# Four residual layers on one Trainium2 core: layer 2's rank products from fp32 operands in column tiles, and gate and up's step 1 begun behind step 0's first two products

## The reference: what is computed

```
x = x + einsum('bsi,boi->bso', x, w0[ids0])                          # layer 0
x = x + x @ W.T + 2 * (h * gates) @ B                                # layer 1, router over 8 experts, rank 16
x = x + x @ weight.T + bias + 0.5 * (x @ A[ids3]) @ lora_B.T         # layer 2, rank 32
gate = x @ Wg.T + 0.5 * (x @ Ag[ids4].T) @ Bg[ids4].T                # layer 3, rank 16
up   = x @ Wu.T + 0.5 * (x @ Au[ids4].T) @ Bu[ids4].T
act  = silu(gate) * up                                               # 1376 columns, padded to 11 blocks of 128
x = x + act @ Wd.T + 0.5 * (act @ Ad[ids4].T) @ Bd[ids4].T
```

## Time and profile before

| | |
|---|---|
| time, median of 3 runs | 288.58 us (288.47 to 288.65) |
| the profiled execution's own time | 288.6 us |
| its span (first to last instruction) | 286.8 us |
| TensorE busy | 279.4 us, 97% of the span |
| VectorE busy | 227.5 us, 79% |
| ScalarE busy | 158.5 us, 55% |
| GpSimd busy | 45.7 us, 16% |
| chain that ended last | 95% TensorE |

### The profile page before, as it was taken

One profiled execution on the slowest core, in us unless ns is written; L12 is line 12 of the kernel. 1 busy time (PEld: TensorE's weight loads), 2 busy tenths in 40 slices (PEclk: granted clock), 3 DMA queues, 4 the chain that ended last, 5 costly groups with the idle time before them and its releaser, 6 DMA issues.

```text
span 286.8 us, 4499 instructions
## 1 busy us (share of the span) xinstructions
PE 279.4 (97%) x1573; PEld 231.2 (81%) x1573; DVE 227.5 (79%) x341; ACT 158.5 (55%) x256; POOL 45.7 (16%) x67
## 2 busy tenths in 40 slices
PE   7899999999999999999999999999999999999993
PEld 7567878888888778888888888888888888888883
DVE  0698897894746999989686785785789999799990
ACT  2688672512425269775746646646667849952110
POOL 1000000000714502514244044044000000000000
PEclk9999999999999999999999999999999999999999
DMA  6999954007603040030270350330291500000043
GB/s 199 371 401 395 400 181 112 0 0 237 204 0 81 22 125 25 10 139 0 65 228 5 100 193 2 110 111 0 73 336 69 152 0 0 0 2 0 0 181 113
DMA packets 19447, 33.28 MB, mean 116 GB/s; under 512 B 2528, under 2 KB 11232, under 8 KB 19040
## 3 DMA queue, kind: packets, MB, share of 16 engines
q1 hardware_dynamic: 19136, 32.47, 33.2%
q10 hardware_dynamic: 288, 0.52, 0.6%
HBM read 30.89 MB, written 2.10 MB: 115 GB/s over the span
## 4 chain that ended last, share of the span: by engine, by line
PE 95%; DMA 2%; DVE 1%; SPq 1%; issue 0%
PE bank L1617 12%; PE bank L1618 12%; PE bank L1619 12%; PE bank L1494 6%; PE bank L1496 6%; PE bank L1495 6%; PE bank L1757 6%; PE bank L1759 6%; PE bank L1760 6%; PE bank L1599 4%; PE bank L1454 3%; PE bank L1471 2%; PE bank L1478 2%; PE bank L1742 2%; DMA w_raw<-in_w 2%; PE bank L1480 2%
## 5 line engine op out<-in xcount | busy, mean ns | idle before, releaser
L619 ACT ACTIVATE part<-bank 128x512 f32<-128x512 f32 x48 | 28.3, 595 | 44.8 <-PE bank L1619 34.7
L1218 DVE TENSOR_TENSOR part<-bank,part 128x512 f32<-128x512 f32 x44 | 29.2, 683 | 1.4 <-PE bank L1599 1.4
L1143 DVE SCALAR_TENSOR_TENSOR bgu_st<-bgu_st,lo_rows,bgu_raw 128x512 fp32r<-128x512 f32 x22 | 17.3, 824 | 12.1 <-ACT bgu_st L619 12.1
L967 DVE TENSOR_TENSOR w_hl<-w_raw,w_hl 128x512 fp32r<-128x512 f32 x31 | 20.0, 687 | 5.6 <-ACT w_hl L619 5.6
L619 ACT ACTIVATE w_hl<-w_raw 128x512 fp32r<-128x512 f32 x31 | 18.6, 622 | 6.1 <-DMA w_raw<-in_w 6.0
L601 POOL TENSOR_TENSOR s_tmp<-wgu_raw 128x256 f32<-128x256 f32 x11 | 8.4, 762 | 80.7 <-DVE wc_up L967 38.8
L1617 PE MATMUL bank<-xb,wc_gate 128*128 128x512 f32 x48 | 18.9, 394 | 0.0
L1619 PE MATMUL bank<-xb,wc_gate 128*128 128x512 f32 x48 | 18.9, 394 | 0.0
L1618 PE MATMUL bank<-xb,wc_gate 128*128 128x512 f32 x48 | 18.8, 392 | 0.0
L1599 PEld LDWEIGHTS bank<-t_st,bgu_st 128*128 128x128 f32 x88 | 14.7, 188 | 2.8 <-DVE t_st L1208 0.3
L619 ACT ACTIVATE xb<-x_f 128x512 fp32r<-128x512 f32 x14 | 8.8, 626 | 13.4 <-DVE x_f L1088 9.4
(11 more groups left out here) (227 smaller groups left out, 792.1 us busy)
## 6 DMA issues: line engine op xcount, KB each, us to landing
wgu_raw<-in_wgu SPq DMA_DIRECT2D x11, 512.0 KB, 4.4
bgu_raw<-in_bgu SPq DMA_DIRECT2D x40, 128.0 KB, 2.7
w_raw<-in_w SPq DMA_DIRECT2D x16, 256.0 KB, 10.9
w_raw<-in_w SPq DMA_DIRECT2D x3, 1024.0 KB, 6.8
w_raw<-in_w SPq DMA_DIRECT2D x6, 512.0 KB, 10.4
wd_raw<-in_wd SPq DMA_DIRECT2D x4, 704.0 KB, 5.9
x_f<-in_xT SPq DMA_DIRECT2D x6, 256.0 KB, 10.1
bd_raw<-in_bd SPq DMA_DIRECT2D x8, 128.0 KB, 2.8
```

The source lines that it names most:

```text
L619: return act.activation(dst, src, ACT.Copy)
L967: return dve.tensor_tensor(dst, src, hi.bitcast(F32), ALU.subtract)
L1143: return dve.scalar_tensor_tensor(out=st, in0=st.bitcast(F32), scalar=lo_rows16[:, 0:1], in1=raw, op0=ALU.mult, op1=ALU.add)
L1218: dve.tensor_tensor(dst[:], bank[4 * (n % 2) + b][:], dst[:], ALU.add).then_inc(c_added, 1)
```

## The change

In layer 2, `thin` becomes `thin2`: fp32 operands (a2_raw and x_f, no split), 32 columns for each of the four sequences in column tiles of their own, 16 matmuls for each half, as `thin3` has it. It waits for x_sum and not for the split of x; that wait (x_lo) now stands behind it, ahead of `base(2,h,0)`. The selection matmul becomes `spread2`: four fp32 matmuls of 128 columns with a matrix t2_sel that POOL builds. ACT's copy into uv becomes a copy of 128 x 128 (`t2_copy`); its copy of sel_r, the split of A on ACT and DVE, and DVE's two subtractions into uv fall away. POOL's memset of t3_st waits for l2_tm to reach 2 (both halves of `thin2` done), and the load of ad_raw for t2_done.

In gate and up, p1(1) and p2(1) move up to stand right behind p2(0). In ACT's and DVE's queues the operations of step 1's weights and xt(2) move ahead of the copies of layer 3's ranks.

```diff
@@ gpsimd
             pool.wait_ge(l0_tr, B)
-            pool.wait_ge(w12_lo, nth["a2"])
+            pool.memset(t2_sel[:], 0.0).then_inc(t2_sel_step, 1)
+            pool.wait_ge(t2_sel_step, 1)
+            pool.wait_ge(sel_in, 16)
+            for j in range(HB):
+                rows = slice(32 * j, 32 * j + 32)
+                pool.tensor_copy(t2_sel[rows, j], sel_raw[rows, 2 * P:3 * P]).then_inc(t2_sel_step, 1)
+            pool.wait_ge(t2_sel_step, 1 + HB)
             pool.wait_ge(main_done, 8)
...
-            pool.wait_ge(sel_copied, 1)
+            pool.wait_ge(l2_tm, H)
             pool.wait_ge(hi_lo_copied, 1)
             pool.memset(t3_st[:].bitcast(F32), 0.0).then_inc(t3_zeroed, 1)
@@ scalar
-            split_hi("a2")
...
-            def t2_uv_high(h):
+            def t2_copy(h):
                 act.wait_ge(l2_tm, h + 1)
-                high(uv[0:2 * R2, h * HT:(h + 1) * HT], bank[h][0:2 * R2]).then_inc(t2_uv_hi, 1)
+                high(t2_sb[:, h], bank[h][:, 0:S]).then_inc(t2_copied, 1)
...
-            act.wait_ge(sel_in, 16)
-            high(sel_r[:], sel_raw[:, 2 * P:3 * P]).then_inc(sel_copied, 1)
...
             copy_part(0, 0)
+            xt_high(2)
+            wc_high(1, 1)
+            wc_high(1, 2)
+            copy_part(1, 0)
             t3_high(0)
             copy_part(0, 1)
-            xt_high(2)
             t3_copy(1)
-            wc_high(1, 1)
-            wc_high(1, 2)
             bgu_high(0, 1)
-            copy_part(1, 0)
             xt_high(3)
@@ vector
-            split_lo("a2")
...
-            t2_uv_low(0)
...
-            t2_uv_low(1)
...
-            t3_low(0)
-            bgu_low(0, 1)
             for part_of in (1, 2):
                 wc_low(1, part_of)
             xt_low(2)
+            t3_low(0)
+            bgu_low(0, 1)
             xt_low(3)
@@ tensor
-            def thin(h, a_hl, x):
+            def thin2(h):
+
+                pe.wait_ge(x_sum, number(1, h, C - 1) + 1)
+                for c in range(C):
+                    for j in range(HB):
+                        b = HB * h + j
+                        ins = pe.matmul(bank[h][32 * j:32 * j + R2, 0:S], a2_raw[:, b, c], x_f[:, b, c],
+                                        start=(c == 0), stop=(c == C - 1))
+                ins.then_inc(l2_tm, 1)
+
+            def spread2(h):
+
+                pe.wait_ge(t2_copied, h + 1)
                 for j in range(HB):
+                    ins = pe.matmul(bank[2 + h][:, j * S:(j + 1) * S], t2_sel[:, j], t2_sb[:, h], start=True, stop=True)
+                ins.then_inc(t2_done, 1)
...
             for h in range(H):
+                thin2(h)
                 pe.wait_ge(x_lo, x_splits(1, h, C - 1))
-                thin(h, a2_hl, xa).then_inc(l2_tm, 1)
                 base(2, h, 0)
...
             pe.wait_ge(x_sum, number(2, 1, C - 1) + 1)
+            p1(1)
+            p2(1)
             sum_ranks(0)
             p5(0)
             thin3(1)
-            p1(1)
-            p2(1)
             p6(0)
             sum_ranks(1)
             lora_w(0)
```

More of the change, by code:

```diff
@@ L109, in bass_four_residual_layers @@
         a2_raw = at("a2_raw", o_tp + 4 * KB, [B, C, R2])
-        a2_hl = at("a2_hl", o_ad, [B, C, 2, R2], F32R)
+        t2_sel = at("t2_sel", o_ad, [HB, P])
+        t2_sb = at("t2_sb", o_ad + 2 * KB, [H, S])
         b2_raw = at("b2_raw", o_bst + 5 * KB, [D])
         b2_st = at("b2_st", o_bst, [D], F32R)
-        uv = at("uv", o_w0 + 16 * KB, [T], F32R)
         t2_st = at("t2_st", o_w0 + 12 * KB, [T], F32R)
@@ L171, in bass_four_residual_layers @@
         sel_raw = at("sel_raw", o_tp, [4 * P + 1])
-        sel_r = at("sel_r", o_misc, [P], F32R)
         hi_lo = own("hi_lo", [1])
@@ L245, in bass_four_residual_layers @@
         t3_sel_step = sem("t3_sel_step")
-        sel_copied, t2_uv_hi, td_copied = sem("sel_copied"), sem("t2_uv_hi"), sem("td_copied")
+        t2_sel_step, t2_copied, td_copied = sem("t2_sel_step"), sem("t2_copied"), sem("td_copied")
         bgu_hi, silu_done = sem("bgu_hi"), sem("silu_done")
@@ L255, in bass_four_residual_layers @@
         t2_lo, t3_lo = sem("t2_lo"), sem("t3_lo")
-        t2_uv_lo, hi_lo_copied = sem("t2_uv_lo"), sem("hi_lo_copied")
+        hi_lo_copied = sem("hi_lo_copied")
         bgu_ready, act_mul = sem("bgu_ready"), sem("act_mul")
@@ L299, in x_f_tokens @@
             return x_f[:, cols.start // S:cols.stop // S, o]
-        splits = [f"w1_{o}" for o in range(C)] + ["b1", "a2"] + [f"w2_{o}" for o in range(C)] + ["b2"]
+        splits = [f"w1_{o}" for o in range(C)] + ["b1"] + [f"w2_{o}" for o in range(C)] + ["b2"]
         nth = {name: i + 1 for i, name in enumerate(splits)}
@@ L308, in split_views @@
                 return b1_raw[:], b1_hl[:, 0], b1_hl[:, 1]
-            if name == "a2":
-                return a2_raw[:], a2_hl[:, :, :, 0], a2_hl[:, :, :, 1]
             if name == "b2":
@@ L315, in split_views @@
             return raw[:, o], hl[:, 0, o], hl[:, 1, o]
-        split_source = {"b1": (b1_in, 16), "a2": (a2_in, 16 * B), "b2": (b2_in, 16)}
+        split_source = {"b1": (b1_in, 16), "b2": (b2_in, 16)}
         for o in range(C):
@@ L529, in _ @@
             load_wgu(4)
-            sp.wait_ge(l2_tm, 2)
+            sp.wait_ge(t2_done, H)
             for b in range(B):
@@ L571, in _ @@
             pool.wait_ge(t3_sel_step, 1)
-            pool.wait_ge(sel_in, 16)
             for g in range(2):
@@ L729, in xt_high @@
                 high(xt_views(k)[0], tx[k][:]).then_inc(xt_hi, 1)
-            t2_uv_high(0)
-            act.wait_ge(sel_in, 16)
-            high(sel_r[:], sel_raw[:, 2 * P:3 * P]).then_inc(sel_copied, 1)
+            t2_copy(0)
             t2_high(0)
@@ L736, in _ @@
                 x_high(2, 0, o)
-            t2_uv_high(1)
+            t2_copy(1)
             wc_high(0, 0)
@@ L1125, in _ @@
             dve.wait_ge(bias_in, 16)
[L1127 to L1130, removed]
             def t2_low(h):
@@ L1533, in _ @@
                     lora1(h, o)
-            def thin(h, a_hl, x):
-                for j in range(HB):
[L1538 to L1545, removed]
+            def thin2(h):
[8 more added lines that the diff above has]
+                pe.wait_ge(t2_copied, h + 1)
+                for j in range(HB):
+                    ins = pe.matmul(bank[2 + h][:, j * S:(j + 1) * S], t2_sel[:, j], t2_sb[:, h], start=True, stop=True)
+                ins.then_inc(t2_done, 1)
             def delta2(h, o):
@@ L1551, in delta2 @@
                           t2_st[:, h * HT:(h + 1) * HT], start=False, stop=True).then_inc(main_done, 1)
-            pe.wait_ge(w12_lo, nth["a2"])
+            pe.wait_ge(a2_in, 16 * B)
             for h in range(H):
+                thin2(h)
                 pe.wait_ge(x_lo, x_splits(1, h, C - 1))
-                thin(h, a2_hl, xa).then_inc(l2_tm, 1)
                 base(2, h, 0)
[L1559 to L1562, removed]
+                pe.wait_ge(t2_sel_step, 1 + HB)
+                spread2(h)
                 base(2, h, 1)
```

## The result

The changed kernel takes 294.02 us (median of 4 executions, 292.94 to 294.27) against 288.52 us before (median of 4): a ratio of 1.0184, 95% interval 1.0169 to 1.0199, about 5.3 us slower by the ratio (5.5 us between the medians). All four executions are slower than any of before.

A forecast was written before the change was run, and what follows sets the result against it. TensorE, never idle in the changed stretch, was taken as the bound. sum_ranks(1) starting 4.0 us late, with layer 2's 0.3 us only lengthening the wait, on 288.6 us makes 292.6 us; range 290.9 to 294.8 us.

The forecast's parts named there:

- The bound, and that a reordering has nothing to fill: TensorE, busy all 37.00 us from 75 to 112 us, bounds the kernel; reordering its queue can only add a wait.
- The place and the mechanism: Gate and up: TensorE waits at sum_ranks(1) from 111.5 us for t3_low(0), which has three subtractions newly ahead on DVE.
- The size of the wait: At sum_ranks(1): TensorE waits 4.3 us, to 115.8 us, so the second spreading starts 4.0 us later than before.
- the shift ahead of the chain: POOL's moved memset delays form_s(0), ACT's split and DVE's chain behind it by 0.76 us.
- The upper end of 1.4 us: The shift if POOL's memset also waits for a whole DVE operation of 0.7 us; gives 293.3 us.
- Layer 2 on TensorE: thin2 and spread2 in place of the old groups gain 0.2 to 0.4 us for both halves, taken as 0.3.
- the clock's fall: Rival: TensorE's clock drops to half speed behind the wait, costing up to 2.8 us, 295.4 us at most; chance 0.20.
- the likeliest case: The wait at sum_ranks(1) without a fall of the clock: 292.6 us, range 291.2 to 293.3; chance 0.66.
- Its reading of the start: At the program's start, fp32 passes of 0.20 us, against 0.11 us later, show TensorE at 1.2 instead of 2.4 GHz.
- The rest follows as before: Behind sum_ranks(1), everything to the program's end keeps its earlier timing, so its delay of 4.0 us passes on whole.
- rival 2: Gate and up: the wait is there but well shorter, DVE being ahead of the sum; 290 to 291.2 us, chance 0.08.
- Just in time, so no wait yet: p1(1), due at about 103.8 us, needs the last addition to x_f, shifted to 103.7 us; TensorE doesn't wait there.

The follow-up runs named there:

- Run 3: The changed kernel with ACT's and DVE's queues in the order of before, TensorE keeping p1(1) and p2(1) early: 289.84 us, ratio 1.0048.
- run 4: The changed kernel with TensorE's order of before; ACT and DVE keep the new queues: 293.1 us, ratio 1.0159.
- run 2: The kernel before with only the reordering on TensorE, ACT and DVE, layer 2 as before: 292.97 us, ratio 1.0136.
- run 5: The changed kernel with 16 more matmuls on TensorE, moving operand all zeros, in the place of the wait: 291.55 us, ratio 1.0110.
- run 6: The changed kernel with xt_low(2) moved behind the ranks' low parts of half 0 on DVE: 290.6 us, ratio 1.0081.
- run 1: The changed kernel without its reordering: layer 2's part alone, with the memset of t3_st behind l2_tm: 288.25 us, ratio 1.0002.
- run 7: As run 1, but POOL's clearing of the rank tile stands behind step 0's weight sums: 287.56 us, ratio to before 0.9971.
- runs 2 and 9: Run 2, and the kernel before with only POOL's clearing of the rank tile moved behind step 0's weight sums: 287.92 us, ratio 0.9985.

## Why the prediction was right, and what it had wrong

**The bound, and that a reordering has nothing to fill: right.** TensorE waited nowhere in this stretch before; the change gave it a wait.

**The place and the mechanism: right.** TensorE comes to the second spreading at 111.5 us as said and waits for `t3_low(0)`. Run 3 (queues back: no wait there) and run 4 (TensorE's order back: 3.3 us of it) show that the three subtractions and four ACT operations ahead of the ranks make the wait, and run 2 that layer 2 isn't needed for it.

**The size of the wait: 3.67 us late instead of 4.0.** (TensorE idles 3.75 us; the prediction had 4.3.) The chain from `form_t(2)` to the end of `t3_low(0)` was summed as 8.56 us (107.24 to 115.8) and took 8.44 (106.87 to 115.31). The spreading then starts 0.15 us behind its end, which the sum left out. What was too large is the shift ahead of the chain: 0.76 us by the sum, 0.38 measured. The memset began and lasted as said (87.35, 1.82 us), but `form_s(0)` took 2.92 us and not 3.41: its third operation took 0.73 us and not 1.19, since (argued from the timelines, not tried) it no longer fell together with DVE's subtraction of step 0's weights. The upper end of 1.4 us took the Trainium skill's lock of the port pair (SBUF — State Buffer, Terms) to hold for the memset. The trace shows no such delay: the memset took 1.82 us with DVE's subtractions beside it and 1.81 us without. Nor does that page (SBUF: two separate sides) ask for one: it says that a DVE operation with two SBUF inputs contends only with a GpSimd operation that reads SBUF, and a memset reads nothing.

**Layer 2 on TensorE: right.** `thin2` costs 73.54 - 72.20 - 0.23 = 1.11 us and 0.1 us ahead of it, `spread2` 77.18 - 76.06 - 0.23 = 0.89 us:

```profile
72.20 1.08 PE L1532 MATMUL bank<-x_f,a_raw 128*32 128x128 f32 x32
...
73.54 0.40 PE L1486 MATMUL bank<-xa,w_hl 128*128 128x512 f32 x1
...
76.06 1.05 PE L1540 MATMUL bank<-t_sb,t_sel 128*128 128x128 f32 x8
...
77.18 0.40 PE L1486 MATMUL bank<-xa,w_hl 128*128 128x512 f32 x1
```

The two halves together gain 0.2 us, the low end of 0.2 to 0.4.

**The step that failed: the clock's fall was priced as a rival at 0.20, and it is what happened,** in all four executions of the changed kernel. 294.02 us lies above the likeliest case's 291.2 to 293.3; the forecast's range holds it since it reached into this rival. The likeliest case, the wait alone, measures 291.5 us (run 5); the fall brings 1.7 us (run 6), and in some executions 1.1 us more: the changed kernel has a span of 290.7 and 290.8 us where the mean clock is 0.994, and 291.9 us where it is 0.988, the mean of run 4's profiled execution with its longer low stretch. The rival's own price of up to 2.8 us fits the sum. Its reading of the start, that a pass of 0.20 us is one at the low level, is borne out: at a granted clock of 0.50 8 passes of that shape took 1.70 us in run 4, 0.21 us each. That a gap throttles the clock again is the rule cited from the Trainium skill (TensorE: Matmul & The Clock Gate, HAM oscillation), and the traces agree: 0.50 in the windows behind the wait. How long a gap does it was open, and it should have been weighed higher.

**Some luck in the number.** "The rest follows as before" didn't hold at the end: behind the last addition the span is 1.1 us shorter and outside it lie 0.3 us more. Run 5, with the whole wait and no fall, is at 291.55 us where the sum has 292.6, mainly for this reason: its path is 3.84 us longer than before, close to the 4.0 of the sum. In the changed kernel this end took back a part of what the clock cost. A slip without weight is rival 2's time: it leaves the shift of 0.76 us out, and 113.46 - 111.79 gives 290.3 us and not 290.2.

**"Just in time, so no wait yet": right for p1(1) at 103.93, incomplete as an account of the memset.** The copy `t3_copy(0)`, late by the same 0.38 us, isn't waited for in the changed kernel, since p1(1) and p2(1) stand ahead; with the ranks in their old place it costs TensorE about 0.4 us there and 0.2 us at `lora_y(0)` (run 1 against run 7). Having the memset wait for an event for which the next operation waits too moved it from idle time onto a path.

What stays open is the time behind the last addition. It is 3.2 us in the profiled execution of each of the nine kernels that have layer 2's part and 4.3 us in the three that don't (before, runs 2 and 9), so it goes with layer 2's part or with something that comes along with it; which, no run tells. The kernel before has besides two spans, 0.8 us apart, from one execution to the next, and only the longer was profiled.

## What to carry to other kernels

On an engine that waits for nothing, a group moved forward can only make room for a wait: look which semaphore the next group takes, and which queue feeds it; here the damage was done by four ACT and three DVE operations put ahead of one that TensorE needed first. Price a wait of a few microseconds on TensorE as the wait plus some 1.7 to 2.8 us of half clock, and reckon with the fall already at 2 us (3 of 6 executions here); if the wait can't be avoided, even idle multiplications in it are better than nothing (run 5; real work in their place wasn't tried). And an operation that clears or fills memory belongs behind the operation that shares its event, if its own reader comes much later: with layer 2's part that edit gave 0.7 us (run 1 against run 7). The 287.56 us that came of it are 0.3% under the kernel before, but by the profiled executions nearly all of this lies at the end of the program, whose cause is open.

## What the runs showed of the hardware

The clock's fall depends on the execution, not only on the program: it fell in 3 of 6 executions with a gap of 2.1 us, in 3 of 4 with 3.2 us, in 4 of 4 with 3.3 and in 4 of 4 with 3.7 us, and in 5 of 6 with two gaps of 1.6 and 1.4 us and 0.5 us of work between them (the gaps as profiled in one execution of each). Matmuls with an all-zero moving operand held it at 0.999 to 1.000 in 4 of 4. In the profiled executions the low clock came about 1 us into the work (changed kernel) or 1 us ahead of it, with TensorE still idle (run 4), and lasted to 119.8 and to 121.3 us, 4.3 and 5.9 us behind the restart.

The mean clock of an execution counts the end of the program too. In the kernel before (mean 0.999 in the profiled execution) the window from 286 to 287 us has 0.60, 4 us behind its last matmul, where it costs nothing; run 2's 0.991 holds such a stretch beside the fall behind its wait. Whether a fall cost time is read from the windows in which TensorE works.
